# Four crossed tiles instead of seven on TensorE, a gather released every 5.85 products, and another order of the first block

## The chip, the cores and the metric

One NeuronCore of one Trainium2 chip runs the kernel. The metric is the device time of a whole run in microseconds. The kernel before has a median of 119.67 us over three runs. A difference of about 0.2% is what such a measurement can tell from no change.

## What is computed

A recommender model on 2048 samples: eight embedding fields, a wide part with two crossed fields, and three dense layers.

```python
S = [s0, s1, s2, s3, s4, s5, s6, s7]   # indices of 2048 samples
E = [E0, ..., E7]                      # tables of (125000, 25000, 12500, 375, 375, 1000, 500, 100) x 64
w = [w0, ..., w7]                      # one weight per table row
wide = dense @ Wd_wide                 # dense: 2048 x 13
for si, wi in zip(S, w):
    wide = wide + wi[si]
wide = wide + wc0[S[3] * VOCABS[4] + S[4]]   # 375 x 375 entries
wide = wide + wc1[S[5] * VOCABS[6] + S[6]]   # 1000 x 500 entries
deep_in = jnp.concatenate([dense @ Wd_deep] + [Ei[si] for Ei, si in zip(E, S)], axis=1)
h = jax.nn.relu(deep_in @ W1)          # 576 -> 512
h = jax.nn.relu(h @ W2)                # 512 -> 256
return bias + h @ W3 + wide            # 256 -> 1
```

## The kernel before, in words

The 2048 samples are four blocks of 512, and a block is four tiles of 128. Every large product is made of float32 operands split into a high and a low fp32r part: hi x hi, hi x lo and lo x hi, so three matmuls of 512 columns each (L901, L902, L903 in `product`).

**Two ways to a table row.** Fields 0, 1 and 2 have large tables; GpSimd gathers their rows with indirect DMAs (L388), one for each tile and field: 12 per block, 48 in all (8 `x_pair` for fields 0 and 1, and 4 `x_two` for field 2, per block). The five small tables are looked up on TensorE: VectorE builds a one-hot matrix of the indices (`build_onehot`, L569, 19 chunks of 128 rows per block) and TensorE multiplies the table with it (`look_up`, L842). The weights of the wide part are looked up in the same way by `look_up_wide` (19 narrow matmuls, L854).

**The crossed fields.** The first one, wc0, is a table of 375 x 375. A tile of it can be gathered by GpSimd (L401), or be done on TensorE, a *crossed tile*: six matmuls of 376 columns pick the row (`look_up_crossed`, L893), and VectorE picks the column and sums (`take_crossed`, L684). XTILES = 7 tiles of the 16 go this way, at the places of the table CROSSED, written (block, place). For them TensorE also spreads the row indices (L877, one 128-column matmul a tile). The remaining 9 tiles of wc0 and all 16 of wc1 are gathered, 25 in all.

**When a gather starts.** GpSimd issues its gathers in one fixed order. Those of block 0 start as soon as the indices are there: first four `x_two`, then eight `x_pair` with a memset of 160 columns (`pause`, L376) behind each. All later ones wait for the semaphore `gather_released`. TensorE raises it: `count` adds up the products issued (1 for a 512-column matmul, less for a narrower one), and when a matmul marked free finds the sum above PACED_FROM + PACE x (gathers released so far), 58 + 6.3 n, its end releases one gather. Look-ups' last matmuls, the low-weight matmuls of `product`, turns and the wide look-up are not free.

**The first block.** TensorE starts with five filler matmuls (L1013), spreads the indices of block 0 over the partitions (L826), runs two more fillers (BUSY), and then follows an order written out by hand. ScalarE copies the spread indices (`copy_spread`, L410; field 5's is the fifth, into `idx_bc`), splits the high halves of the tables (L463) and weights (L467), and copies each look-up's result out of PSUM (L429, L430). VectorE computes the low halves of the tables (L579) and weights (L575) between the one-hots. The dense features have a weight product of their own, Wd_deep x W1 (L1030), which `dense` (L958) uses.

**The later blocks** repeat one order in a loop: layer 2, look-ups, layer 1 by groups of 128 input rows, turns of the gathered rows (L866), the crossed tiles at their places. Three PSUM banks (`io_ps`) go round among look-ups, turns, crossed tiles and sums. The last block ends with layer 2 in two halves, the matmuls L997 and L1006, and on VectorE the sum of the crossed gathers (L797), the result of three blocks (L798) and the final add (L801).

## Time and profile before

| | |
|---|---|
| median of three runs | 119.67 us (119.65 to 119.74) |
| the profiled execution, its own time | 119.41 us |
| its span in the profile | 117.6 us |
| TensorE busy | 113.9 us, 97% of the span |
| VectorE, ScalarE, GpSimd busy | 77.2, 57.8, 80.8 us |
| DMA moved | 7.47 MB, 64 GB/s on average |

The profile's times start at the span's start. A row of a timeline has the start, the length, the engine, the source line, the operation, output and input, and in brackets the idle time before it with what ended it. Matmuls overlap: their starts follow each other closer than their lengths tell. The chain of waits is followed back from the last instruction, at each step to what released it.

### The profile page before, as it was taken

The page shows a single profiled execution, that of the slowest core. Times are in us where ns is not written, and L with a number is a line of the kernel's source. Part 1 is how long each engine was busy: PE and PEld are TensorE (multiplying, and loading weights), DVE is VectorE, ACT ScalarE, POOL GpSimd, SP SyncE. Part 2 cuts the span into 40 slices and gives each one's busy share as a digit, 9 for nine tenths or more (in the row PEclk, how much of TensorE's full clock was granted, in tenths as well). Part 3 has the DMA queues.
Part 4 walks back from the last instruction along what each step waited for, and adds up shares of the span by engine and source line. Part 5 has one row for each costly group of instructions (what it writes and reads, how often), then busy time and mean ns, then how long its engine had stood idle before and what let it go on. Part 6 is the DMA issues. An engine that isn't in the chain of part 4 may idle for free.

```text
span 117.6 us, 1749 instructions
## 1 busy us (share of the span) xinstructions
PE 113.9 (97%) x595; PEld 89.0 (76%) x595; DVE 77.2 (66%) x195; ACT 57.8 (49%) x106; POOL 80.8 (69%) x92
## 2 busy tenths in 40 slices
PE   5999999999999999999999999999999999999992
PEld 2757665877887886888888886788888888688892
DVE  3799999948999944929994504847997004534450
ACT  5799977169593251238255052407628052406230
POOL 7578888575787773667777768377777766377630
PEclk9999999999999999999999999999999999999999
DMA  2897954459732343033334442120000000000000
GB/s 72 244 213 268 232 149 85 82 149 279 271 25 20 21 85 27 5 27 25 28 23 71 36 26 23 11 21 3 0 9 0 0 0 0 0 0 0 6 0 3
DMA packets 6073, 7.47 MB, mean 64 GB/s; under 512 B 2748, under 2 KB 3772, under 8 KB 6064
## 3 DMA queue, kind: packets, MB, share of 16 engines
q0 software_dynamic: 2336, 1.61, 17.2%
q1 hardware_dynamic: 3728, 5.74, 14.9%
q8 instruction: 5, 0.08, 0.3%
q14 instruction: 4, 0.03, 0.1%
HBM read 7.32 MB, written 0.03 MB: 62 GB/s over the span
## 4 chain that ended last, share of the span: by engine, by line
PE 88%; DVE 5%; ACT 2%; DMA 2%; issue 0%
PE l_ps L901 18%; PE l_ps L903 18%; PE l_ps L902 18%; PE io_ps L842 12%; PE io_ps L893 6%; PE io_ps L854 4%; DVE onehot L569 3%; PE l_ps L958 3%; PE io_ps L866 2%; PE l_ps L826 2%; DMA idx_raw<-in_index_dram 2%; PE io_ps L983 1%; ACT xt_lo L430 1%; ACT xt_hi L429 1%; PE io_ps L997 1%; PE io_ps L1013 1%
## 5 line engine op out<-in xcount | busy, mean ns | idle before, releaser
L388 POOL DMA_INDIRECT x_pair<-in_rows_dram,idx_gather x32 | 33.5, 1048 | 13.3 <-issue 5.1
L569 DVE TENSOR_SCALAR onehot<-idx_bc,row_id 128x512 fp32r<-128x512 f16 x76 | 33.0, 496 | 2.3 <-PE io_ps L854 2.1
L401 POOL DMA_INDIRECT cross<-in_wc_dram,idx_cross x25 | 24.8, 990 | 10.3 <-issue 4.9
L901 PE MATMUL l_ps<-xt_hi,w_hi 128*128 128x512 f32 x60 | 23.9, 398 | 0.0
L903 PE MATMUL l_ps<-xt_hi,w_lo 128*128 128x512 f32 x60 | 23.6, 393 | 0.0
L902 PE MATMUL l_ps<-xt_lo,w_hi 128*128 128x512 f32 x60 | 23.5, 391 | 0.0
L388 POOL DMA_INDIRECT x_two<-in_rows_dram,idx_gather x16 | 17.6, 1097 | 7.7 <-issue 3.7
L842 PE MATMUL io_ps<-onehot,table_hl 128*128 128x512 f32 x76 | 21.4, 405 | 0.2 <-DVE onehot L569 0.2
L429 ACT CAST xt_hi<-io_ps 64x512 fp32r<-64x512 f32 x20 | 11.6, 579 | 16.2 <-PE io_ps L842 16.0
L842 PEld LDWEIGHTS io_ps<-onehot,table_hl 128*128 128x128 f32 x76 | 14.2, 189 | 5.1 <-issue 1.3
L459 ACT ACTIVATE h<-l_ps 128x512 f32<-128x512 f32 (+2 forms) x10 | 5.0, 512 | 21.5 <-PE l_ps L903 21.5
L901 PE MATMUL l_ps<-h_hi,w_hi 128*128 128x512 f32 (+1 forms) x36 | 13.4, 372 | 0.0
L901 PEld LDWEIGHTS l_ps<-xt_hi,w_hi 128*128 128x128 f32 x60 | 11.3, 188 | 2.8 <-issue 0.5
L903 PE MATMUL l_ps<-h_hi,w_lo 128*128 128x512 f32 (+1 forms) x36 | 13.3, 369 | 0.0
L902 PE MATMUL l_ps<-h_lo,w_hi 128*128 128x512 f32 (+1 forms) x36 | 13.2, 366 | 0.0
L903 PEld LDWEIGHTS l_ps<-xt_hi,w_lo 128*128 128x128 f32 x60 | 11.3, 188 | 2.5
L902 PEld LDWEIGHTS l_ps<-xt_lo,w_hi 128*128 128x128 f32 x60 | 11.3, 188 | 2.4
L590 DVE TENSOR_TENSOR xt_lo<-io_ps,xt_hi 128x512 fp32r<-128x512 f32 x4 | 2.8, 692 | 15.2 <-ACT xt_hi L443 15.2
L623 DVE SCALAR_TENSOR_TENSOR h_lo<-l_ps,h_hi 128x512 fp32r<-128x512 f32 x16 | 10.1, 682 | 3.9 <-ACT h_hi L450 3.9
L430 ACT CAST xt_lo<-io_ps 64x512 fp32r<-64x512 f32 x20 | 11.6, 582 | 0.5
L450 ACT ACTIVATE h_hi<-l_ps 128x512 fp32r<-128x512 f32 x16 | 8.8, 598 | 4.0 <-PE l_ps L903 3.6
L684 DVE SCALAR_TENSOR_TENSOR taken<-col_id,cross_col,io_ps 128x376 f32<-128x376 f32 x7 | 4.2, 602 | 8.6 <-PE io_ps L893 8.6
(101 smaller groups left out, 140.7 us busy)
## 6 DMA issues: line engine op xcount, KB each, us to landing
idx_bc<-idx_dram SPq DMA_DIRECT2D x3, 640.0 KB, 7.2
w_sb<-in_w_dram SPq DMA_DIRECT2D x4, 256.0 KB, 4.6
dense_x<-in_dense_x_dram SPq DMA_DIRECT2D x4, 154.0 KB
table<-in_wc_rows_dram SPq DMA_DIRECT2D x1, 564.0 KB, 3.8
x_pair<-in_rows_dram,idx_gather POOLq DMA_INDIRECT x32, 3.5
w_sb<-in_w_dram SPq DMA_DIRECT2D x1, 512.0 KB, 4.3
cross<-in_wc_dram,idx_cross POOLq DMA_INDIRECT x25, 2.4
table<-in_small_dram SPq DMA_DIRECT2D x1, 256.0 KB, 3.5
```

The source lines that it names most:

```text
L388: nc.gpsimd.indirect_dma_start(out=x_two[:, t // 2, t % 2 * ROW:(t % 2 + 1) * ROW] if f == 2 else x_pair[:, t, f * ROW:(f + 1) * ROW], out ...
L401: nc.gpsimd.indirect_dma_start(out=cross[:, c, t:t + 1], out_offset=None, in_=wc[c], in_offset=bass.IndirectOffsetOnAxis(ap=idx_cross[:, c ...
L429: nc.scalar.copy(xt_hi[b % 2][to, g, :], bank[0:D, :]).then_inc(io_act, 1)
L430: nc.scalar.copy(xt_lo[b % 2][to, g, :], bank[D:2 * D, :]).then_inc(io_act, 1)
L450: nc.scalar.activation(h1_hi[:, m, :], l1_ps[m][:], ACT.Relu).then_inc(l1_high, 1)
L569: nc.vector.tensor_scalar(onehot[:, CHUNK0[i] + c, :], idx_bc[:, b % (BLOCKS - 1), i, :], row_id[:, c:c + 1], None, ALU.is_equal).then_inc ...
L623: nc.vector.scalar_tensor_tensor(out=h1_lo[:, m, :], in0=l1_ps[m][:], scalar=0.0, in1=h1_hi[:, m, :].bitcast(f32), op0=ALU.max, op1=ALU.su ...
L842: last = count(nc.tensor.matmul(io_bank(use)[:], table_hl[:, c, :], onehot[:, c, :], start=c == CHUNK0[i], stop=ends), free=not ends)
L893: last = count(nc.tensor.matmul(io_bank(use)[:, 0:XPAD], row_onehot[:, c, t % BT * P:(t % BT + 1) * P], cross_hl[:, part, c, :], start=c + ...
L901: count(nc.tensor.matmul(dst, w_hi, a_hi, start=start, stop=False), columns, free=True)
L902: count(nc.tensor.matmul(dst, w_hi, a_lo, start=False, stop=False), columns, free=True)
L903: return count(nc.tensor.matmul(dst, w_lo, a_hi, start=False, stop=stop), columns)
```

## The change

- XTILES goes from 7 to 4. The crossed tiles stand at (1, 3), (2, 1), (2, 3), (3, 1); those at (1, 1), (1, 2), (2, 0), (2, 2) are gone and (2, 1) is new. Three more tiles of wc0 are gathered, so there are 28 cross gathers.
- The gathers are released by other numbers: the eight `x_pair` gathers of block 0 too, at 9 + 5.6 n products, and the rest every 5.85 products. The memsets between the first gathers are gone.
- In block 0 the two fillers before the first look-up are gone; the dense weights' product is issued before look-up (0, 1), and its inputs are loaded earlier; ScalarE's copy of W1's group 2 stands behind the third index copy; VectorE computes the low half of W1's group 3 behind the last one-hots, and then the parts of the wide weights; TensorE takes group 3's matmuls with high weights first (`layer1_weights_low_last`); `dense(0)` is issued before `turn(0, 0)`.

The diff, cut to its core:

```diff
--- before.py
+++ after.py
@@ -45,35 +45,32 @@
-BUSY = 2
...
-XTILES = 7
+XTILES = 4
...
-PAUSE = 160
-PACE, PACED_FROM = 6.3, 58
...
-CROSSED = {(1, 1): [0], (1, 2): [1], (1, 3): [2], (2, 0): [3], (2, 2): [4], (2, 3): [5],
-           (3, 1): [6]}
+PACE, FIRST_PACE, PACED_FROM = 5.85, 5.6, 9
+
+FIRST_RELEASED = BT * 2
+RELEASED = FIRST_RELEASED + (BLOCKS - 1) * BT * NG + NX * TILES - XTILES
...
+CROSSED = {(1, 3): [0], (2, 1): [1], (2, 3): [2], (3, 1): [3]}
...
-RELEASED = (BLOCKS - 1) * BT * NG + NX * TILES - XTILES
@@ -303,10 +299,10 @@
             table_part(0)
-            w1_part(2)
-            table_part(1)
             sp.dma_start(wd_rep[:], wd_rep_t).then_inc(wd_loaded, 16)
             sp.dma_start(w1d_sb[:], w1[0:D, :]).then_inc(wd_loaded, 16)
+            table_part(1)
+            w1_part(2)
             table_part(2)
@@ -369,20 +365,14 @@
-            def pause(n, columns):
-
-                if n:
-                    pool.wait_ge(paused, n)
-                nc.gpsimd.memset(pause_sb[:, 0:columns], 0.0).then_inc(paused, 1)
-
...
-                            if b > 0:
+                            if b > 0 or f != 2:
                                 released += 1
                                 pool.wait_ge(gather_released, released)
...
-                            if b == 0 and f != 2:
-                                pause(pauses, PAUSE)
-                                pauses += 1
@@ -475,9 +462,9 @@
-            weight_high(2)
             table_high_part(1)
             copy_spread(2)
+            weight_high(2)
             copy_spread(3)
@@ -732,11 +719,8 @@
             table_low_part(2)
+            build_onehot(0, 4, range(4, CHUNKS[4]))
             w1_low_part(1)
-            build_onehot(0, 4, range(4, CHUNKS[4]))
-            w1_low_part(2)
-            wdense_low()
-            turned_lo(0, 1)
...
+            w1_low_part(2)
+            turned_lo(0, 1)
+            wdense_low()
             dense_low(0)
@@ -813,10 +800,13 @@
+            def release_at(n):
+                return PACED_FROM + FIRST_PACE * min(n, FIRST_RELEASED) + PACE * max(n - FIRST_RELEASED, 0)
+
...
-                if free and work[0] >= PACED_FROM + PACE * released[0] and released[0] < RELEASED:
+                if free and released[0] < RELEASED and work[0] >= release_at(released[0]):
@@ -915,15 +905,28 @@
+            def layer1_weights_low_last(g):
+
+                pe.wait_ge(io_act, act_count(IO_AT["look", 0, 3]))
+                pe.wait_ge(w1_high, W1_ORDER.index(g) + 1)
+                for m in range(M1):
+                    for part in (xt_hi[0], xt_lo[0]):
+                        count(nc.tensor.matmul(l1_ps[m][:], w1_hi[:, g, m * P:(m + 1) * P], part[:, g, :],
+                                               start=False, stop=False), free=True)
+                pe.wait_ge(w1_low, W1_ORDER.index(g) + 1)
+                for m in range(M1):
+                    count(nc.tensor.matmul(l1_ps[m][:], w1_lo[:, g, m * P:(m + 1) * P], xt_hi[0][:, g, :],
+                                           start=False, stop=False), free=True)
@@ -1022,24 +1025,23 @@
-            keep_busy(BUSY, io_ps[1])
             look_up(0, 0)
-            look_up(0, 1)
             pe.wait_ge(wd_loaded, 32)
             pe.wait_ge(row_index_ready, 1)
             nc.tensor.matmul(l2_ps[0:NROWS, :], wd_rep[:], w1d_sb[:], start=True, stop=True).then_inc(wdense_done, 1)
+            look_up(0, 1)
             look_up(0, 2)
...
-            layer1(0, 3)
+            layer1_weights_low_last(3)
             look_up_wide(0)
             layer1(0, 1)
             look_up(1, 0)
+            dense(0)
             turn(0, 0)
-            dense(0)
             look_up(1, 1)
```

GpSimd's queue from the first gathers to the row gathers of block 1, before:

```order
L371 MEMSET ones 128x1
L388 DMA x_two<-in_rows_dram,idx_gather 128x65 x4
L388 DMA x_pair<-in_rows_dram,idx_gather 128x65
L376 MEMSET pause_sb 128x160
...
L388 DMA x_pair<-in_rows_dram,idx_gather 128x65 x8
L388 DMA x_two<-in_rows_dram,idx_gather 128x65 x4
```

And after:

```order
L367 MEMSET ones 128x1
L378 DMA x_two<-in_rows_dram,idx_gather 128x65 x4
L378 DMA x_pair<-in_rows_dram,idx_gather 128x65 x16
L378 DMA x_two<-in_rows_dram,idx_gather 128x65 x4
L378 DMA x_pair<-in_rows_dram,idx_gather 128x65 x8
```

The memsets are gone, and the sixteen row gathers of blocks 0 and 1 wait alike for `gather_released`.

VectorE's queue around the last one-hots of block 0, before (L569 one-hots, L579 and L575 low halves of tables and weights):

```order
L569 TENSOR_SCALAR onehot<-idx_bc,row_id 128x512 x5
L579 TENSOR_TENSOR table_hl<-table,table_hl 128x8x64
L575 TENSOR_TENSOR w_lo<-w_sb,w_hi 128x512
L569 TENSOR_SCALAR onehot<-idx_bc,row_id 128x512 x4
L575 TENSOR_TENSOR w_lo<-w_sb,w_hi 128x512
L610 TENSOR_TENSOR wdense_hl<-l_ps,wdense_hl 13x512
L595 TENSOR_TENSOR xt_lo<-io_ps,xt_hi 64x2x128 x2
```

And after (L556, L566 and L562 are the same three lines):

```order
L556 TENSOR_SCALAR onehot<-idx_bc,row_id 128x512 x5
L566 TENSOR_TENSOR table_hl<-table,table_hl 128x8x64
L556 TENSOR_SCALAR onehot<-idx_bc,row_id 128x512 x4
L562 TENSOR_TENSOR w_lo<-w_sb,w_hi 128x512
L727 CAST look_w_parts<-look_w 128x19
L728 TENSOR_TENSOR look_w_rest<-look_w,look_w_parts 128x19
L729 CAST look_w_parts<-look_w_rest 128x19
L730 TENSOR_TENSOR look_w_parts<-look_w_rest,look_w_parts 128x19
L562 TENSOR_TENSOR w_lo<-w_sb,w_hi 128x512
```

The four last one-hots now follow the table's low half directly, and the weights' low half and the four steps on the wide weights come behind them.

TensorE's queue in block 0, from the index spreads to the second layer-1 products, before:

```order
L826 MATMUL l_ps<-ident,idx_look 128x128 x4
L1013 MATMUL io_ps<-zero 128x512 x2
L842 MATMUL io_ps<-onehot,table_hl 128x512 x6
L1030 MATMUL l_ps<-w1d_sb,wd_rep 77x512
L842 MATMUL io_ps<-onehot,table_hl 128x512 x4
L912 MATMUL l_ps<-xt_hi,w_hi 128x512 x2
```

And after:

```order
L816 MATMUL l_ps<-ident,idx_look 128x128 x4
L832 MATMUL io_ps<-onehot,table_hl 128x512 x3
L1031 MATMUL l_ps<-w1d_sb,wd_rep 77x512
L832 MATMUL io_ps<-onehot,table_hl 128x512 x7
L902 MATMUL l_ps<-xt_hi,w_hi 128x512 x2
```

The two fillers went out, and the dense weights' product stands between the first three look-up matmuls and the other seven.

## Rows read from the trace of the kernel before

**Rows 1.** The page: busy us, share of the span and instructions of the engines.
```profile
PE 113.9 (97%) x595; PEld 89.0 (76%) x595; DVE 77.2 (66%) x195; ACT 57.8 (49%) x106; POOL 80.8 (69%) x92
```

**Rows 2.** The chain of waits, 5 to 16.5 us: start, us, engine, output, line.
```profile
8.67 0.58 ACT xt_hi L429
...
9.88 0.59 ACT idx_bc L410
...
10.49 2.06 DVE onehot L569 x4
...
13.14 0.60 DVE w_lo L575
...
15.81 0.51 PE io_ps L842
```

**Rows 3.** The timeline of TensorE in block 0: start, us, line, operation, tiles, count.
```profile
3.66 1.01 PE L826 MATMUL l_ps<-ident,idx_look 128*128 128x128 f16 x8 [0.15 <-DVE idx_look L554]
...
8.04 1.08 PE L1030 MATMUL l_ps<-w1d_sb,wd_rep 64*77 64x512 f32 x2
9.05 1.19 PE L842 MATMUL io_ps<-onehot,table_hl 128*128 128x512 f32 x4
...
19.10 1.32 PE L854 MATMUL io_ps<-onehot,look_w_parts 128*32 128x512 bf16 x19
...
23.94 0.60 PE L866 MATMUL io_ps<-ident,x_pair 128*128 128x128 f32 x4
...
26.01 0.72 PE L912 MATMUL l_ps<-xt_hi,w_hi 128*128 128x512 f32 x2
```

**Rows 4.** VectorE: its timeline, and L569 alone from 10.4 to 15.9 us (ns).
```profile
4.90 2.47 DVE L569 TENSOR_SCALAR onehot<-idx_bc,row_id 128x512 fp32r<-128x512 f16 x6
...
18.71 0.25 DVE L746 TENSOR_TENSOR look_w_parts<-look_w_rest,look_w_parts 128x19 bf16<-128x19 f32 x1
...
L569 DVE TENSOR_SCALAR onehot<-idx_bc,row_id x8: 469/530/772, 10.5 to 15.0; 128x512 fp32r<-128x512 f16 x8
```

**Rows 5.** The timeline of GpSimd: a pause, the last row gather of block 0, and the end.
```profile
12.29 0.42 POOL L376 MEMSET pause_sb<- 128x160 f32 x1
...
20.36 0.97 POOL L388 DMA_INDIRECT x_pair<-in_rows_dram,idx_gather  x1 [0.16 <-issue]
...
102.75 0.94 POOL L401 DMA_INDIRECT cross<-in_wc_dram,idx_cross  x1 [2.02 <-PE l_ps L958]
...
111.77 0.94 POOL L401 DMA_INDIRECT cross<-in_wc_dram,idx_cross  x1 [0.31 <-PE l_ps L901]
```

**Rows 6.** The chain of waits at the index spreads and at a crossed tile.
```profile
35.85 0.41 PE io_ps L877 x7
...
44.12 1.04 PE io_ps L893 x6
```

**Rows 7.** The page's groups of gathers: busy, mean ns, idle before.
```profile
L388 POOL DMA_INDIRECT x_pair<-in_rows_dram,idx_gather x32 | 33.5, 1048 | 13.3 <-issue 5.1
...
L401 POOL DMA_INDIRECT cross<-in_wc_dram,idx_cross x25 | 24.8, 990 | 10.3 <-issue 4.9
...
L388 POOL DMA_INDIRECT x_two<-in_rows_dram,idx_gather x16 | 17.6, 1097 | 7.7 <-issue 3.7
```

**Rows 8.** Who waited for whom: us in total, times, longest.
```profile
DVE taken L684 <- PE io_ps L893: 8.6, 5, 2.3
...
PEld io_ps L866 <- DMA x_pair<-in_rows_dram,idx_gather: 0.2, 1, 0.2
```

**Rows 9.** The line L401: from a cross gather's start to its landing.
```profile
DMA to landing us min/median/max: 2.3/2.4/3.3
```

**Rows 10.** The timeline of VectorE at the end.
```profile
114.22 0.18 DVE L797 TENSOR_TENSOR wide_cross<-wide_bias,cross 128x16 f32<-128x16 f32 x1 [0.34 <-DMA cross<-in_wc_dram,idx_cross]
114.43 0.17 DVE L798 TENSOR_TENSOR result<-wide_cross,deep 128x12 f32<-128x12 f32 x1
115.52 0.16 DVE L801 TENSOR_TENSOR result<-wide_cross,io_ps 128x4 f32<-128x4 f32 x1 [0.92 <-PE io_ps L1006]
```

15 lines of the change are left out of this document (7 added, 8 removed).

## The prediction

> **What bounds the kernel now.** I read the busy shares first. TensorE is busy for 113.9 of 117.6 us [rows 1]: there is hardly a hole to fill, so time comes off there only with its work. The chain of waits says the same, with one exception. From 6 to 16 us it does not run on TensorE, although TensorE reads as busy: it runs from the first look-ups over ScalarE's copies (the second pair starts at 8.67) and the last index copy (L410, 9.88) to VectorE, which then builds eight one-hots (L569) with two low halves (L579, L575) between them; TensorE's last look-up matmul waits for the last one-hot, at 15.81 [rows 2]. From there on TensorE's own stream is the path up to the final add at 115.52 [rows 10]. GpSimd's gathers are a second, nearly full queue: 48 row gathers and 25 cross gathers [rows 7]. The profiled run took 119.41 us, 1.8 more than its span and 0.26 less than the median of 119.67; I take the change from the span and apply it to the median.
>
> **Part 1, three crossed tiles less on TensorE.** One crossed tile is six matmuls and holds the chain for 1.04 us [rows 6]. Three fewer give 3 x 1.04 = 3.12 us. Seven index spreads in one stretch hold it for 0.41 us [rows 6], so three fewer give 0.18. Nothing else waits behind them: in each place where a tile goes, the next group of TensorE (a layer-1 group, the wide look-up, look-up (2, 1)) has inputs that were ready earlier, since VectorE waited there for the crossed product and not the reverse (8.6 us over five waits, [rows 8]). The tile that moves to place (2, 1) costs what it did. Sum: **-3.3 us**; bounds -3.1 (the spreads hidden) and -3.5 (three switches of shape more, of some 0.05 each, go as well).
>
> **Part 2, the start of block 0.** Its steps, in order of time:
> - The two filler matmuls go. Look-up (0, 0) can start behind the spreads: 3.66 + 21 x 0.107 is about 5.9. Its first matmul, of 512 columns, still runs at the lower clock, 0.43 us: up to there eight 128-column matmuls take 1.01 us, later seven hold the chain for 0.41 [rows 3, 6], which is the lower (1.2 GHz) against the upper level (2.4 GHz). The clock should rise by 6.4 as today, so its third matmul starts at about 6.62.
> - The product of the dense weights (L1030) now comes before look-up (0, 1). It holds the queue for 9.05 - 8.04 = 1.01 us [rows 3]. It starts at 6.62 + 0.32 = 6.94, look-up (0, 1) starts at 7.95 and its last matmul is done at 8.90 (four of them take 1.19 us, so three about 0.95). ScalarE's copies of it started at 8.67 [rows 2] and now start near 8.93: **+0.27**, and the copy L410, for which VectorE waits, comes that much later. The order of ScalarE's earlier copies is turned round without a change of their sum. Bounds 0 and +0.5.
> - The low half of W1's group 3 (L575, 0.60 us in the chain, [rows 2]) moves behind the last one-hot: **-0.60**. TensorE does not need it at once, since the new order takes eight matmuls of high weights first (8 x 0.23 = 1.8 us). This is safe.
> - The memsets on GpSimd between the gathers go. Undisturbed, six one-hots take 2.47 us, or 0.40 each beside the next start; in the critical stretch the longest takes 772 ns, and the median 530 [rows 4]. The first four of the stretch end at 12.55, just over the start of a memset at 12.29 [rows 5], and the second four have such a meeting too; the first six one-hots ran beside gathers and show nothing of the kind. Four one-hots that start 0.40 apart end after 3 x 0.40 + 0.47 = 1.67 us instead of 2.06 [rows 2], and the second four are as long, since they end just before 15.81: up to 2 x 0.39 = -0.78. I take **-0.65**, because a gather may still touch one; bounds 0 and -0.78.
> - Behind that, layer 1's group 1 waits less: the wide look-up started only at 19.10, behind its weights' parts, which were done at 18.96 [rows 3, 4]; they are now built earlier: **-0.1**.
> - The eight row gathers of block 0 are now released by TensorE instead of being issued between memsets. Counting products (0.25 for a wide matmul), the eighth is released by the first matmul behind the wide look-up, at about 19.6, and starts near 20.0. A gather that started at 20.36 had landed when the turn began at 23.94, with some 0.2 us of waiting [rows 3, 8], so this takes 3.4 to 3.6 us; the new one lands at 23.4 to 23.7, and the turn, now behind the dense product, comes up at about 23.7. **+0.1**; bounds 0 and +0.5.
>
> Sum of part 2: 0.27 - 0.60 - 0.65 - 0.1 + 0.1 = **-1.0 us**. Layer 1 of group 0, at 26.01 today [rows 3], should start near 25.0. All at the good end gives -1.4, all at the bad end +0.3.
>
> **Part 3, the gathers behind.** Three cross gathers more, 28 instead of 25, all on GpSimd, and paced at 5.85 products. Undisturbed, a gather with the 0.31 before it takes 0.94 + 0.31 = 1.25 us, and with the disturbed ones among them 1.29 (cross) to 1.40 (x_two) [rows 5, 7]. A release comes every 5.85 x 0.23 = 1.35 us and more where uncounted work lies between, so the queue can just follow. In the last block TensorE frees none during the wide look-up and the turns; the queue runs dry and starts again at 102.75, today with eight gathers to go, of which the eighth starts at 111.77 [rows 5]. Now nine are to go: on today's axis the ninth starts at 102.75 + 8 x 1.25 = 112.75 and has landed 2.4 us later [rows 9], at 115.15. VectorE's L797 waits for that; it and L798 need 0.21 and about 0.1 before the engine is free [rows 10], so 115.5, where the final add starts today at 115.52 because of TensorE. The cover of 0.9 us is used up. **+0.05**; bounds 0 and +0.9 (a landing of 3.3 us, [rows 9]).
>
> **Sum.** -3.3 - 1.0 + 0.05 = -4.25 us. From the profiled 119.41 that is 115.2, from the median **115.4 us**.
>
> **A rule weighed.** GpSimd's gathers run beside VectorE's one-hots, and their mean is 1.05 us over 32, against 0.94 for one alone [rows 5, 7]. The Trainium skill (SBUF — State Buffer, section Who interferes with whom) says that a VectorE instruction in a two-port mode and a GpSimd instruction exclude each other, and the same page (A bandwidth-pool intuition that's wrong) gives some 620 ns alone against 3100 ns overlapped for such a DMA. By that rule the memsets' removal frees VectorE, as I assume; but it also speaks against adding gathers. By its figure, an estimate, 72 gathers would need over 220 us, so the trace disagrees with its size.
>
> **Rivals.**
> - *A, the start gives nothing.* The dense product ahead of look-up (0, 1) delays VectorE by 0.5, the one-hots stay long for another reason (gathers now start where memsets did), and the turn waits 0.5 for its rows: 0.5 - 0.6 - 0.1 + 0.5 = +0.3. For it: ScalarE's copies are gapless from 8.67 on, so whatever they start late reaches VectorE whole [rows 2]. Against: the memset's coincidence with the long one-hot. Time 119.67 - 3.3 + 0.3 = 116.7; half-way, with the memsets' part missing only, 116.0.
> - *B, the last gather ends the kernel.* The ninth gather starts or lands late by 0.5 to 1 us more: 115.9 to 116.4. For it: its cover is gone by my own sum. Against: landings have a median of 2.4.
> - *C, the clock.* Without fillers the rise to the full level comes later. Each 512-column matmul then takes 0.43 instead of 0.23 and the dense product twice 1.01; through ScalarE's chain that costs 1 to 1.5 us: 116.4 to 116.9. Against: look-ups fill the place of the fillers without a hole.
> - *D, slower than before: GpSimd becomes the bound from end to end.* 72 released gathers start at about 10.0. By kind they take 32 x 1.35 + 12 x 1.40 + 28 x 1.29 = 96.1 us [rows 7], so the last would end at 106, before TensorE. The kernel gets slower than today only if the last one starts after 112.9 of the span, which needs a mean of (112.9 - 10.0) / 71 = 1.45 us against 1.33. At 1.48 the last starts at 115.1 and the time is about 121.9. It needs every gather lengthened by 0.15. The rule weighed above would point this way.
> - *E, the change doesn't do what it says.* The counts of instructions rule that out for the crossed tiles.
>
> **How the numbers follow.** Forecast 0.62; A, half or whole, 0.18; B 0.10; C 0.05; D 0.02; an even better start 0.03. The likeliest is 115.4. The low end takes the good end of part 2 and of part 1: 119.67 - 3.5 - 1.4 = 114.8. The high end takes in A and most of C: 116.8. About 0.2% is what a measurement here can tell from no change: slower by more only with D, 0.02; within it 0.01; faster 0.97.
>
> **What would show it.** In the new profile: 24 matmuls of crossed tiles at 1.04 us per six; the last look-up matmul of block 0 near 14.8; no one-hot above 0.6 us between 10 and 16 us; group 0 of layer 1 near 25.0; the span near 113.3; the final add released by TensorE with L797 just ahead of it. A last look-up matmul near 15.5 means that the memsets were not the cause (A). A wait of the final add for L797 or a DMA means B. 128-column or 512-column matmuls at half speed behind 7 us mean C. GpSimd without idle time from 10 us on means D.

## The result, and the profile after

The changed kernel takes 116.8 us (median of 6 runs, 115.8 to 119.7) where the kernel before takes 119.7: the ratio is 0.968 [0.967, 0.970]. The ratio leaves out runs that were disturbed or over 1.5% above the fastest, and here that matters: of the twelve runs of the changed kernel in two sittings seven lie between 115.4 and 117.0 us and five between 117.6 and 119.7, while the kernel before stays within 119.4 and 120.3. Forecast was 115.4 with a range of 114.8 to 116.8. The direction holds, and the median lies on the upper end of the range; as the runs scatter over 3.9 us and the second sitting gave 116.84, that it falls inside is partly luck. 115.4 is the best run, not the median. The profiled run took 117.59 us, 1.8 more than its span of 115.8.

The page after: the engines, and the three groups of gathers (line, engine, operation, tiles, count; busy us, mean ns; idle time before).

```profile
PE 110.4 (95%) x572; PEld 85.2 (74%) x572; DVE 73.1 (63%) x186; ACT 57.2 (49%) x105; POOL 84.7 (73%) x87
...
L378 POOL DMA_INDIRECT x_pair<-in_rows_dram,idx_gather x32 | 35.2, 1100 | 12.3 <-issue 7.0
L388 POOL DMA_INDIRECT cross<-in_wc_dram,idx_cross x28 | 27.8, 992 | 8.5 <-issue 4.6
...
L378 POOL DMA_INDIRECT x_two<-in_rows_dram,idx_gather x16 | 19.6, 1228 | 5.9 <-issue 3.0
```

TensorE lost 3.5 us of work [rows 1], as it should. GpSimd's gathers take 6.7 us more than before, 82.6 against 75.9, although three gathers at 0.99 make only 3.0: the others have become longer too, x_pair 1100 ns against 1048, x_two 1228 against 1097 [rows 7]. TensorE's timeline in block 0 and at the end, after:

```profile
13.13 0.44 PE L856 MATMUL io_ps<-ident,x_two 128*128 128x128 f32 x2 [0.22 <-DMA x_two<-in_rows_dram,idx_gather]
13.33 2.11 PE L832 MATMUL io_ps<-onehot,table_hl 128*128 128x512 f32 x8
15.28 0.40 PE L924 MATMUL l_ps<-xt_hi,w_hi 128*128 128x512 f32 x1
...
18.10 1.32 PE L844 MATMUL io_ps<-onehot,look_w_parts 128*32 128x512 bf16 x19
...
24.21 0.66 PE L856 MATMUL io_ps<-ident,x_pair 128*128 128x128 f32 x4 [0.18 <-DMA x_pair<-in_rows_dram,idx_gather]
25.29 1.20 PE L832 MATMUL io_ps<-onehot,table_hl 128*128 128x512 f32 x3 [0.42 <-ACT xt_lo L417]
26.32 0.62 PE L902 MATMUL l_ps<-xt_hi,w_hi 128*128 128x512 f32 x2
...
111.07 0.95 PE L1000 MATMUL io_ps<-ones,wide_deep_look 128*128 128x1 f32 x8
```

The wide look-up starts at 18.10 instead of 19.10 [rows 3]: the microsecond is won there. Eight us later it is gone: layer 1 of group 0 starts at 26.32 instead of 26.01 [rows 3], because the turn at 24.21 waited for its gathers and the look-up behind it for ScalarE (how much each took is told below, at the run with the memsets). The second loss stands at the end. VectorE's timeline there, then the last entries of the chain of waits (start, us, engine, output, line):

```profile
113.42 0.17 DVE L784 TENSOR_TENSOR wide_cross<-wide_bias,cross 128x16 f32<-128x16 f32 x1 [2.56 <-DMA cross<-in_wc_dram,idx_cross]
...
113.72 0.15 DVE L788 TENSOR_TENSOR result<-wide_cross,io_ps 128x4 f32<-128x4 f32 x1
```

```profile
109.75 1.01 POOL cross L388
110.76 0.30 issue
111.07 2.33 DMA cross<-in_wc_dram,idx_cross
```

In the kernel before the final add waited 0.92 us for TensorE and L797 0.34 for a DMA [rows 10]. Now L784, the same operation, waits 2.56 us for the last cross gather, and the final add follows it at once. Where TensorE ends the kernel, the add starts 1.44 us after L1000 (110.61 and 112.05 in the run with the split row, below; L997, the same, at 114.09 and the add at 115.52 before), so TensorE would have allowed 111.07 + 1.44 = 112.51. The add started at 113.72: **1.21 us** are lost to the gather.

So the difference of spans adds up: TensorE's stretch from layer 1 of group 0 to L1000 fell from 114.09 - 26.01 = 88.08 to 111.07 - 26.32 = 84.75, **-3.33**; the start of that stretch **+0.31**; the end **+1.21**. Together -1.81, and the span went from 117.6 to 115.8.

### The profile page after: what moved, and what is told of

Read it like the earlier page. It is cut to its first block, busy times and chain, and to the rows that moved or that the text cites. A ratio compares the mean times of both kernels' runs of the same rounds, so it can differ in the third digit from the quotient of the medians.

```text
span 115.8 us, 1680 instructions
## 1 busy us (share of the span) xinstructions
PE 110.4 (95%) x572; PEld 85.2 (74%) x572; DVE 73.1 (63%) x186; ACT 57.2 (49%) x105; POOL 84.7 (73%) x87
## 4 chain that ended last, share of the span: by engine, by line
PE 72%; DMA 16%; SPq 4%; ACT 2%; POOL 2%; issue 1%; DVE 0%; DVEq 0%
PE l_ps L891 16%; PE l_ps L893 16%; PE l_ps L892 15%; PE io_ps L832 11%; DMA w_sb<-in_w_dram 5%; DMA idx_bc<-idx_dram 4%; DMA idx_dram<-row_idx 4%; PE io_ps L883 4%; PE io_ps L844 3%; PE l_ps L961 2%; DMA cross<-in_wc_dram,idx_cross 2%; PE io_ps L856 2%; POOL cross L388 2%; PE io_ps L986 2%; SPq L296 1%
## 5 line engine op out<-in xcount | busy, mean ns | idle before, releaser
L378 POOL DMA_INDIRECT x_pair<-in_rows_dram,idx_gather x32 | 35.2, 1100 | 12.3 <-issue 7.0
L388 POOL DMA_INDIRECT cross<-in_wc_dram,idx_cross x28 | 27.8, 992 | 8.5 <-issue 4.6
L556 DVE TENSOR_SCALAR onehot<-idx_bc,row_id 128x512 fp32r<-128x512 f16 x76 | 31.7, 482 | 2.2 <-PE io_ps L844 2.0
L378 POOL DMA_INDIRECT x_two<-in_rows_dram,idx_gather x16 | 19.6, 1228 | 5.9 <-issue 3.0
L891 PE MATMUL l_ps<-xt_hi,w_hi 128*128 128x512 f32 x56 | 22.3, 398 | 0.0
L893 PE MATMUL l_ps<-xt_hi,w_lo 128*128 128x512 f32 x56 | 22.0, 393 | 0.0
L892 PE MATMUL l_ps<-xt_lo,w_hi 128*128 128x512 f32 x56 | 21.9, 392 | 0.0
L891 PEld LDWEIGHTS l_ps<-xt_hi,w_hi 128*128 128x128 f32 x56 | 10.5, 188 | 2.7 <-issue 0.4
L893 PEld LDWEIGHTS l_ps<-xt_hi,w_lo 128*128 128x128 f32 x56 | 10.5, 188 | 2.3
L892 PEld LDWEIGHTS l_ps<-xt_lo,w_hi 128*128 128x128 f32 x56 | 10.5, 188 | 2.3
L417 ACT CAST xt_lo<-io_ps 64x512 fp32r<-64x512 f32 x20 | 11.7, 583 | 0.5
L891 PEld LDWEIGHTS l_ps<-h_hi,w_hi 128*128 128x128 f32 x36 | 6.8, 189 | 1.4 <-issue 0.4
```

Source lines behind the costliest of these rows:

```text
L378: nc.gpsimd.indirect_dma_start(out=x_two[:, t // 2, t % 2 * ROW:(t % 2 + 1) * ROW] if f == 2 else x_pair[:, t, f * ROW:(f + 1) * ROW], out ...
L388: nc.gpsimd.indirect_dma_start(out=cross[:, c, t:t + 1], out_offset=None, in_=wc[c], in_offset=bass.IndirectOffsetOnAxis(ap=idx_cross[:, c ...
L417: nc.scalar.copy(xt_lo[b % 2][to, g, :], bank[D:2 * D, :]).then_inc(io_act, 1)
L556: nc.vector.tensor_scalar(onehot[:, CHUNK0[i] + c, :], idx_bc[:, b % (BLOCKS - 1), i, :], row_id[:, c:c + 1], None, ALU.is_equal).then_inc ...
L891: count(nc.tensor.matmul(dst, w_hi, a_hi, start=start, stop=False), columns, free=True)
L892: count(nc.tensor.matmul(dst, w_hi, a_lo, start=False, stop=False), columns, free=True)
```

## The experiments

Three questions: what each half of the change is worth alone, what eats the microsecond of the start, and what makes the last gather late. The time of the kernel before beside each was 119.6 to 119.7 us.

**The change once more.** No edit.

> The changed kernel once more, for a second profile. Theory 1 (a chain of long gathers, one of 3.70 us and one of 2.87 us, filled GpSimd's queue in the first profile, and the last gather set the end 1.95 us late): an execution without such gathers has a span near 113.9 us and the final add released by TensorE; one with them ends behind the last cross gather. Theory 2 (the pace itself is too fast for the queue): the last gather sets the end in every execution, also with no gather above 1.5 us. Ratio to before 0.966 to 0.971.

116.84 us (115.44 to 118.57), ratio 0.972 [0.967, 0.977]. In its profile (115.88 us, span 114.1) group 0 starts at 25.75, the last gather at 109.24 and L1000 at 110.56, 84.81 behind group 0. The add comes 1.43 us after L1000, and no gather takes over 1.92 us, as theory 1 has it. The 84.8 us come again, the two other terms don't: they vary from run to run.

**The crossed tiles alone.**

```diff
-XTILES = 7
+XTILES = 4
-PACE, PACED_FROM = 6.3, 58
+PACE, PACED_FROM = 5.85, 53.8
-CROSSED = {(1, 1): [0], (1, 2): [1], (1, 3): [2], (2, 0): [3], (2, 2): [4], (2, 3): [5],
-           (3, 1): [6]}
+CROSSED = {(1, 3): [0], (2, 1): [1], (2, 3): [2], (3, 1): [3]}
```

> The kernel before with the new tile table and the new pace alone (XTILES 4, release base 53.8 and 5.85 products); its first block and its memsets stay. Prediction: -3.3 us of TensorE and +0.05 to +0.9 at the tail, so 116.4 us, ratio 0.973. Rival (first block gives nothing, all of the gain is the tiles): ratio 0.968, 115.9 us.

118.34 us (116.9 to 119.2), ratio 0.985 [0.981, 0.989]: about half of the 3.3 us, and slower than both expectations. TensorE's stretch is as short as it should be, 111.51 - 26.72 = 84.79 us. Its timeline, then the end of VectorE's:

```profile
26.72 0.73 PE L911 MATMUL l_ps<-xt_hi,w_hi 128*128 128x512 f32 x2
...
111.51 0.95 PE L996 MATMUL io_ps<-ones,wide_deep_look 128*128 128x1 f32 x8
```

```profile
113.91 0.18 DVE L796 TENSOR_TENSOR wide_cross<-wide_bias,cross 128x16 f32<-128x16 f32 x1 [2.60 <-DMA cross<-in_wc_dram,idx_cross]
...
114.20 0.15 DVE L800 TENSOR_TENSOR result<-wide_cross,io_ps 128x4 f32<-128x4 f32 x1
```

The add could have come at 111.51 + 1.44 = 112.95 and came at 114.20: the last gather takes back 1.25 us. The other 0.7 are the start of group 0, 26.72 here and 26.01 before with the same code, which is that run's. In this kernel alone 2.4 to 2.9 us of each run lie outside the span, 1.8 in all others; that takes another 0.6 to 1 us and is not explained.

**The new first block alone.** Seven tiles and the old spacing of later gathers, the rest of the diff.

> The kernel before with the new first block alone: XTILES 7, the old tile table, the old pace of 6.3 from product 58 for the later gathers. Prediction: -1.0 us, 118.7 us, ratio 0.992. Rival (W2's load lands late, at 22.4 us in the first profile of the changed kernel, and takes all of it back): 119.7 us, ratio 1.000.

120.34 us (118.8 to 122.6), ratio 0.999 [0.996, 1.002]. The ratio is the rival's, its reason is not: layer 2's weights reach ScalarE at 20.64 here. The wide look-up starts at 17.91, and then the turn of block 0 waits. TensorE's timeline, and the stretches around it (each engine's busy us and count; PEclk is the granted clock, 1.00 the upper level of 2.4 GHz and 0.50 the lower of 1.2):

```profile
22.76 1.08 PE L962 MATMUL l_ps<-dense_hl,wdense_hl 77*128 77x512 f32 x4
26.48 0.86 PE L857 MATMUL io_ps<-ident,x_pair 128*128 128x128 f32 x4 [2.64 <-DMA x_pair<-in_rows_dram,idx_gather]
26.99 1.63 PE L833 MATMUL io_ps<-onehot,table_hl 128*128 128x512 f32 x3
28.42 1.05 PE L903 MATMUL l_ps<-xt_hi,w_hi 128*128 128x512 f32 x2
```

```profile
26.00:28.00 2.00, 1.52 (x7) 1.32 (x7) 0.01 (x1) 0.58 (x1) 0.35 (x1) 0.70 0.55 30
28.00:30.00 2.00, 2.00 (x6) 1.60 (x5) 1.62 (x3) 1.16 (x2) 0.94 (x1) 0.50 0.75 228
```

TensorE idles 2.6 us, the clock falls to the lower level at 26.8 and comes back at 30.2, and two matmuls take 1.05 us where they take 0.62 after. (The Trainium skill, TensorE: Matmul & The Clock Gate, section HAM oscillation — how this bites in real kernels, says that a wait for a DMA can send the clock back to the lower level; this trace agrees.) A stretch of 3.4 us at the lower level in a span of 120.8 is a mean clock of 0.986. The four slowest of these 14 runs, 121.6 to 122.6 us, have just that mean, and so have, at 0.985, the two slowest without the three gathers and the slowest at spacing 5.4 (both below, 118.7 to 118.9 us); the three slowest of the changed kernel have 0.975 to 0.981. The mean alone does not tell the place, though. The kernel with breaks (below) has 0.984 in its profile and waited only 0.30 us at the turn: its clock is at the lower level from 112.8 us to the end, behind TensorE's last matmul, while the add waits for the last gather. All but one of these slowest runs had no profile. That they wait at the turn is inferred, and is likely only where no late gather ends the kernel: here and without the three gathers.

Why the gathers are late shows on GpSimd, here the last three of block 0:

```profile
19.02 1.49 POOL L379 DMA_INDIRECT x_pair<-in_rows_dram,idx_gather  x1 [0.30 <-issue]
20.82 0.95 POOL L379 DMA_INDIRECT x_pair<-in_rows_dram,idx_gather  x1 [0.30 <-issue]
22.07 1.78 POOL L379 DMA_INDIRECT x_pair<-in_rows_dram,idx_gather  x1 [0.30 <-PE l_ps L892]
```

The eighth starts at 22.07, not near 20.0 as forecast, and takes 1.78 us beside VectorE's w_lo of 1024 columns.

**The same, with the gathers of block 0 released by nothing.**

```diff
-                            if b > 0 or f != 2:
+                            if b > 0:
                                 released += 1
-            work, released = [0.0], [0]
+            work, released = [0.0], [FIRST_RELEASED]
```

> The kernel before with the new first block alone (seven tiles, old spacing of later gathers), and the eight x_pair gathers of block 0 released by nothing: GpSimd issues them back to back behind the x_two ones. The new first block alone had come to 120.3 us (ratio 0.9988 of before), with TensorE waiting 2.64 us for those gathers at its turn of block 0 and then 3.4 us at the lower clock. Theory A (the order of the first block is worth what was predicted, about 1 us, and TensorE's releases give it back, because a released gather that meets VectorE's one-hots is too late for the turn): no wait over 0.3 us at the turn of block 0, layer 1's first step of group 0 begins at 25.0 to 25.6 us (26.01 before), full clock throughout, time 118.5 to 119.2 us, ratio 0.990 to 0.996. Theory B (the new order itself is worth nothing: look-up 1 and the weights that it brings forward wait for other loads instead): the turn without a wait, but group 0 at 25.8 to 26.3 us and the time 119.4 to 120.0 us, ratio 0.998 to 1.003.

119.01 us, ratio 0.996 [0.993, 0.998]. The twelve runs fall into two heaps: nine at 118.7 to 119.2, three at 120.0 to 120.1. The profile caught one of the three:

```profile
25.34 0.66 PE L857 MATMUL io_ps<-ident,x_pair 128*128 128x128 f32 x4 [1.36 <-DMA x_pair<-in_rows_dram,idx_gather]
```

No wait over 0.3 us was expected. Here the eighth gather started at 20.96 and took 2.02 us, since the back-to-back gathers at 12.6 and 14.4 had met one-hots too (1.48 and 1.80). The wait of 1.4 is the distance of the heaps, 1.2. The nine are 0.8 us below the kernel before, which would be the worth of the new order when the turn waits little; none of them was profiled, so that is inferred from the distance. Their time is theory A's, but a free issue does not by itself mend the wait. These runs come from another sitting than those of the new first block alone.

**The memsets put back** behind block 0's x_pair gathers, these released by nothing, everything else as changed.

```diff
+                            if b == 0 and f != 2:
+                                if pauses:
+                                    pool.wait_ge(paused, pauses)
+                                nc.gpsimd.memset(pause_sb[:, 0:160], 0.0).then_inc(paused, 1)
+                                pauses += 1
```

> The changed kernel with the memsets of 160 columns back behind block 0's eight x_pair gathers, and these gathers not released by TensorE; all the rest as changed. If the memsets lengthen the one-hots: two one-hots of some 0.77 us again between 10 and 16 us, the last look-up matmul of block 0 0.6 to 0.8 us later, and the kernel up to 0.65 us slower than the changed one (ratio to before 0.974). If they do not: same one-hots and the same time within 0.2 us.

116.79 us (116.0 to 117.4), ratio 0.975 [0.971, 0.979]. The one-hots of 10 to 15 us (ns: shortest, median, longest), with the memsets, then after, without:

```profile
L562 DVE TENSOR_SCALAR onehot<-idx_bc,row_id x8: 467/512/772, 10.4 to 14.5; 128x512 fp32r<-128x512 f16 x8
```

```profile
L556 DVE TENSOR_SCALAR onehot<-idx_bc,row_id x9: 469/476/542, 9.9 to 14.0; 128x512 fp32r<-128x512 f16 x9
```

The memsets do lengthen them, and four take 2.0 us again. Yet layer 1 of group 3 starts at 15.39 against 15.28 after, as if only 0.1 of the 0.65 reached TensorE. That pair misleads, because TensorE's turn at 13.13 in the profile of after waited for x_two rows and held up the look-up behind it. From the start of the last index copy, for which VectorE waits, to group 3 it is 6.27 us in the kernel before, 4.93 to 5.41 (mean 5.04) in the ten profiles with the new order and no memsets, and 5.56 and 5.63 in the two with memsets. So the memsets cost TensorE about 0.55 us.

The turn of block 0 has no wait here, and group 0 starts at 25.28, 1.04 before the profile of after. The turn comes 5.76 us behind the wide look-up instead of 6.11, and group 0 1.28 us behind the turn instead of 2.11. So 0.35 of the loss after belong to the gathers and 0.83 to the look-up that waited for ScalarE, which was late with layer 2's weights (more on them at the three edits together). At the end this kernel loses 1.22 us like the changed one: L1006, the same as L1000, starts at 110.04 and the add at 112.70.

**Released by nothing, without memsets.** The two edits that released block 0's gathers above (`if b > 0` and `released` from FIRST_RELEASED on), in the changed kernel.

> The changed kernel with block 0's eight x_pair gathers neither released by TensorE nor spaced by memsets. If their release is what makes the turn wait (0.16 and 0.18 us in two profiles, 2.64 us in the one of the first block alone): they end by about 20 us instead of 22, the turn starts behind the dense product with no wait, and layer 1 of group 0 starts at 25.2 instead of 25.8; ratio to the changed kernel 0.997. If the gathers then meet the one-hots of 10 to 15 us and lengthen them: those one-hots above 0.5 us, and no gain.

116.82 us (115.6 to 118.4), ratio 0.970 [0.965, 0.974]. No wait at the turn, group 0 at 25.59. Yet the span is 115.0: L1000 starts at 110.33, which allows the add at 111.77, and it came at 112.93. So a good start alone is not enough; the last gather, at 110.33, takes 1.16 us.

**Three cross gathers less.** The last three of the second crossing are left out (their columns are zero).

> The changed kernel without its last three cross gathers (three tiles of wc1 are left out of the sum and read as zero); everything else as changed, so GpSimd's queue ends three gathers, 3.75 us, earlier. Theory 1 (the spread and the median above the fast runs come from the last gather landing late): all runs close together at the fast level, 115.5 to 116.0 us, ratio 0.967, and the final add released by TensorE. Theory 2 (the spread comes from the first block's loads and turn): the spread stays, 115.5 to 119.

117.15 us (115.7 to 118.9), and the spread stays, as theory 2 has it. Now nothing waits for a gather at the end:

```profile
111.73 0.17 DVE L785 TENSOR_TENSOR wide_cross<-wide_bias,cross 128x16 f32<-128x16 f32 x1
...
113.46 0.16 DVE L789 TENSOR_TENSOR result<-wide_cross,io_ps 128x4 f32<-128x4 f32 x1 [1.35 <-PE io_ps L1010]
```

But the turn of block 0 waited 1.34 us and group 0 started at 27.27. Each cause suffices for a run above 117.

**Releases closer together.**

```diff
-PACE, FIRST_PACE, PACED_FROM = 5.85, 5.6, 9
+PACE, FIRST_PACE, PACED_FROM = 5.4, 5.6, 9
```

> The changed kernel with later gathers released every 5.4 products instead of 5.85. Theory 1: the last release comes 0.45 x 63 = 28 products, 6.5 us, earlier, so GpSimd works with no idle time from block 1 on and has 1 to 2 us more at its end to take up long gathers: median 116.0 to 116.4 us. Theory 2 (the queue is full anyway, and earlier releases bring nothing): 116.8 us.

116.53 us (115.4 to 118.9), between the two theories; the ratio of 0.976 [0.972, 0.980] shows no gain over the changed kernel. The profile has the shortest span of all, 113.6: last gather at 108.79, add at 111.51, exactly where TensorE allows it (110.08 + 1.44 = 111.52).

**Why the last gather is late.** VectorE and GpSimd around 48 us in the changed kernel:

```profile
48.17 3.25 DVE L556 TENSOR_SCALAR onehot<-idx_bc,row_id 128x512 fp32r<-128x512 f16 x8
```

```profile
47.29 0.94 POOL L378 DMA_INDIRECT x_pair<-in_rows_dram,idx_gather  x1 [0.30 <-PE l_ps L961]
48.54 3.70 POOL L378 DMA_INDIRECT x_pair<-in_rows_dram,idx_gather  x1 [0.30 <-issue]
52.54 0.95 POOL L378 DMA_INDIRECT x_pair<-in_rows_dram,idx_gather  x1 [0.30 <-PE l_ps L892]
```

The gather starts 0.37 us into an unbroken row of eight one-hots and takes 3.70 us, until 0.8 after the row. Another, 1.7 us into the row at 35.70, took 2.87. The longest in the kernel before is 1.79. (The Trainium skill, SBUF — State Buffer, section Who interferes with whom, has the one that comes second blocked for the other's whole instruction, and the same page, section A bandwidth-pool intuition that's wrong, gives 620 against 3100 ns. The prediction set that figure aside, because the mean of before was 1.05 us. The excess of this one gather, 2.8 us, is near the page's 2.5, an estimate from its two figures. But a single one-hot lasts 0.48 us, so a block for one instruction doesn't give it, and as a mean over all gathers the figure doesn't hold.) From 48.54 on GpSimd has no idle time but the 0.30 between gathers, and it never runs dry. In the last block, after:

```profile
99.77 0.94 POOL L388 DMA_INDIRECT cross<-in_wc_dram,idx_cross  x1 [0.30 <-PE l_ps L961]
...
111.07 0.94 POOL L388 DMA_INDIRECT cross<-in_wc_dram,idx_cross  x1 [0.30 <-issue]
```

Before, there were 2.02 us of idle time ahead of 102.75 [rows 5]. A gather takes 1.25 us and a release comes every 1.35, so each of the some 45 gathers behind 52 us gives back a tenth of a microsecond at most. The profiles bear this out. In the four with both long gathers the last one starts 84.7 to 84.8 us behind group 0, in the four with neither 83.4 to 83.5, and in the one with the 3.7 alone and closer releases 83.5. The difference, 1.3 us, is about one gather, and it makes the 1.2 us lost at the end.

**Small breaks in the rows.** Behind every second one-hot of blocks 1 to 3 a VectorE addition of one column:

```diff
+                    if b > 0 and c % 2 == 1:
+                        nc.vector.tensor_tensor(gap_sb[:, n:n + 1], wd_scratch[:, 0:1], wd_scratch[:, 1:2], ALU.add)
```

> The changed kernel with a tensor_tensor of one column on VectorE behind every second one-hot of blocks 1 to 3, so that the rows of eight one-hots are no longer one behind the other. Theory 1 (a gather that begins its write inside such a row is locked out until the row ends: 37.41 to 40.28 and 48.54 to 52.24 us in the first profile): no gather above 1.6 us in these rows, median at 115.6 to 116.2 us, little spread. Theory 2 (long gathers come from the DMA side or from chance): gathers of 2.8 and 3.7 us remain and the time is that of the changed kernel, 116.8 us.

119.33 us, ratio 0.994 [0.991, 0.998]: the gain is nearly gone. The gather is as long as ever (47.60, 3.77 us), though it starts 0.19 us ahead of its row, and another joins it (74.54, 3.91). In the profile the add came at 114.47, 2.5 us after TensorE allowed it. The additions start before the one-hot ahead of them has ended (48.58 and 48.66), and VectorE has no idle time in the row, so the run doesn't test a row with real holes.

```profile
47.60 3.77 POOL L379 DMA_INDIRECT x_pair<-in_rows_dram,idx_gather  x1 [0.30 <-issue]
```

**The row split by a wait.**

```diff
                 if b + 2 < BLOCKS:
+                    dve.wait_ge(io_full, IO_AT["look", b + 2, 0] + 1)
                     build_onehot(b + 2, 2)
```

> The changed kernel, with one wait added on VectorE in blocks 0 and 1: between the one-hots of look-up 1 and those of look-up 2 of the block after the next (the row of eight at 48.2 to 51.4 us) VectorE waits for TensorE to have filled the bank of that block's look-up 0. The row falls into 3 and 5, as it did in the kernel before, whose fourth tile stood there (2.29 us of waiting between). Theory A (a gather that starts just after VectorE has begun an unbroken row of one-hots is held until the row is over, and the 2.5 us that it loses at 48.5 us are still missing from GpSimd's queue at the end): the gather at about 48.5 us takes at most 1.3 us in place of 3.70, no gather after 40 us takes over 1.5, GpSimd's last gather starts at 109.5 us or earlier (111.07 in the first profile of the changed kernel), and the time is 115.3 to 116.3 us. The gather of 2.87 us at 37.4 stays, since the row of eight at 35.7 is untouched. Theory B (the gather's 3.70 us are memory or queue trouble and have nothing to do with the row): it stays at 3.5 us or more. Theory C (GpSimd catches up anyway, TensorE's releases set the last gather): gathers short, but the last one still at 110.5 to 111.1 us and the time 116.5 to 117. Against both: if the added wait makes VectorE late for the rounded hidden rows at 53.8 us, the kernel is 0.3 to 1 us slower than the changed one.

116.16 us (115.5 to 116.8), ratio 0.971 [0.967, 0.975]; the last gather starts at 109.27 and TensorE ends the kernel again. The time and three of the four numbers of theory A came true, and still the profile does not prove it. The gather that was to stay at 2.87 us took 1.27, though its row was not touched: the backlog was gone before the split row came. VectorE, then GpSimd:

```profile
47.72 1.27 DVE L556 TENSOR_SCALAR onehot<-idx_bc,row_id 128x512 fp32r<-128x512 f16 x3
50.27 2.09 DVE L556 TENSOR_SCALAR onehot<-idx_bc,row_id 128x512 fp32r<-128x512 f16 x5 [1.28 <-PE io_ps L833]
```

```profile
46.34 0.94 POOL L378 DMA_INDIRECT x_pair<-in_rows_dram,idx_gather  x1 [1.34 <-PE l_ps L962]
47.59 1.18 POOL L378 DMA_INDIRECT x_pair<-in_rows_dram,idx_gather  x1 [0.30 <-issue]
```

The gather started 0.13 us before the row, not 0.37 into it, and the second profile of the changed kernel has the same meeting with the row of eight left whole:

```profile
47.66 3.25 DVE L556 TENSOR_SCALAR onehot<-idx_bc,row_id 128x512 fp32r<-128x512 f16 x8
```

```profile
46.28 0.94 POOL L378 DMA_INDIRECT x_pair<-in_rows_dram,idx_gather  x1 [1.37 <-PE l_ps L961]
47.52 1.19 POOL L378 DMA_INDIRECT x_pair<-in_rows_dram,idx_gather  x1 [0.30 <-issue]
```

At this place the length goes with the phase. Where GpSimd had run dry and was released by the dense product (the idle 1.34 and 1.37 us above), the next gather starts 0.13 us ahead of the row and takes 1.2 us: in that profile, in the three with a split row, in the one with three gathers less, in the kernel before and in the two with seven tiles. Where it still had a backlog it starts 0.37 into the row and takes 3.7: in the first profile of the changed kernel, with the tiles alone, with the memsets, released by nothing, and with closer releases, five of five.

That the phase alone decides is not shown, for two reasons. The gather of the kernel with breaks started 0.19 us ahead of its row and took 3.77 all the same. And in the row of eight at 35.7 a gather starts 0.40 us in and takes 1.00, in all thirteen traces but that of the kernel with breaks. Here from the first profile of the changed kernel:

```profile
35.70 3.26 DVE L556 TENSOR_SCALAR onehot<-idx_bc,row_id 128x512 fp32r<-128x512 f16 x8
```

```profile
36.10 1.00 POOL L378 DMA_INDIRECT x_two<-in_rows_dram,idx_gather  x1 [0.30 <-PE l_ps L892]
37.41 2.87 POOL L378 DMA_INDIRECT x_two<-in_rows_dram,idx_gather  x1 [0.30 <-issue]
```

Either 0.03 us make the difference or something else does, such as the kind of gather (x_two here, x_pair at 48.54); no run tells them apart. The backlog in four of the five comes from the gather of 2.87 us at 37.4. That one starts 1.70 us into its row in all four traces that have it, and in nine others, the kernel before among them, a gather starts at the same 1.70 and takes 1.28. So its cause is open; and a split row met by a gather 0.37 us into it was not seen.

**Three edits together:** released by nothing, the row split, and layer 2's weights no longer behind block 1's spread indices:

```diff
-            sp.wait_ge(index_spread[1], 16)
             sp.wait_ge(w1_low, 2)
```

> The changed kernel with three edits together: block 0's x_pair gathers released by nothing; the row of eight one-hots split by a wait for TensorE as in the run beside it; and the load of layer 2's weights issued behind the second low part of layer 1's weights alone, no longer behind the landing of block 1's spread indices. Theory A (the changed kernel lost at three places: the turn of block 0 that waits for released gathers, 0.2 to 3 us; the one-hots that hold a gather, 2.5 us on GpSimd; layer 2's weights that land at 22.4 and make ScalarE late for look-up 1 of block 1, 0.4 to 0.6 us): turn of block 0 with no wait, layer 1's group 0 at 25.0 to 25.4 us, last gather at 109 us or earlier, time 114.6 to 115.4 us, and little spread between runs. Theory B (TensorE's later work sets the end, about 111.8 us for its last product, and an earlier start only moves a wait behind it): 115.6 to 116.5 us. If GpSimd's back-to-back gathers of block 0 collide with the earlier load of layer 2's weights, group 0 stays at 26 us.

116.32 us (115.4 to 117.1). Theory A failed at the turn: 1.39 us of waiting as in the free first block above (gathers of 1.88, 1.80 and 2.02 us), group 0 at 26.92, span 115.3. The last gather started at 110.37, about as late as TensorE's late end could bear. The time is theory B's, but as the start was not earlier, B is not tested. The weights were issued at 15.63 against 15.59 with the wait in the run beside it, so that wait cost nothing. In the first profile of after they reached ScalarE at 22.44, where the thirteen others have 19.2 to 21.0:

```profile
22.44 1.05 ACT L484 CAST w_hi<-w_sb 128x1024 fp32r<-128x1024 f32 x1 [4.35 <-DMA w_sb<-in_w_dram]
```

The load took 6.3 us from issue to landing there and 4.3 in the second profile. ScalarE's copies behind it ran late one after the other, up to `xt_lo` (L417), for which the look-up at 25.29 waited. Why that one load was slow is open.

**Memsets back and the row split.**

> The changed kernel with the memsets back behind the x_pair gathers of block 0, those gathers released by nothing, and the row of eight one-hots split by the wait for TensorE. Each edit alone gave 116.8 and 116.2 us of median (before 119.6), the second with fewer runs over 117 us. Theory A (what scatters the runs of the changed kernel between 115.5 and 119.7 us is the race between GpSimd's gathers and VectorE's rows at two places: the last gather of block 0, for which TensorE's turn waits up to 2.6 us, and the gather held at 48.5 us): both places are mended here, so the turn of block 0 has no wait, layer 1's group 0 begins at 25.1 to 25.5 us, no gather after 40 us takes over 1.5 us, the last one starts by 109.4 us, and the six runs lie within 1.2 us of each other, with their median at 115.4 to 116.2. Theory B (the first block's one-hots, made long again by the memsets, cost what the turn's wait gives back, and the rest of the spread has another cause): median 116.4 to 116.9, with runs over 117.

115.93 us (115.4 to 116.9), ratio 0.970 [0.966, 0.973]: the best median of all. TensorE's timeline and the end of VectorE's:

```profile
24.52 0.60 PE L863 MATMUL io_ps<-ident,x_pair 128*128 128x128 f32 x4
24.88 0.94 PE L839 MATMUL io_ps<-onehot,table_hl 128*128 128x512 f32 x3
25.80 0.73 PE L909 MATMUL l_ps<-xt_hi,w_hi 128*128 128x512 f32 x2
...
110.53 0.95 PE L1007 MATMUL io_ps<-ones,wide_deep_look 128*128 128x1 f32 x8
```

```profile
111.65 0.18 DVE L791 TENSOR_TENSOR wide_cross<-wide_bias,cross 128x16 f32<-128x16 f32 x1 [1.33 <-DMA cross<-in_wc_dram,idx_cross]
...
111.97 0.16 DVE L795 TENSOR_TENSOR result<-wide_cross,io_ps 128x4 f32<-128x4 f32 x1
```

No wait at the turn, and the add is where TensorE allows it (110.53 + 1.44). The median is within theory A's bounds; the spread is 1.4 us where 1.2 was said, one gather behind 40 us took 1.71 where 1.5 was the limit, and group 0 missed its 25.1 to 25.5 by 0.3, as the wide look-up already started at 18.75. Of the 18 runs with a split row none is above 117.1; of the 36 of the other kernels with four tiles and the new first block, breaks left aside, thirteen are. That does not show that the split takes such runs away. All 18 come from other sittings than the 36, their ratios to the kernel before (0.970 to 0.971) are those of the changed kernel (0.968 and 0.972), and the kernel with three gathers less kept its spread although no gather could end it late.

## Why the prediction was right, and where not

- **Part 1, -3.3 us: right to 0.05.** From layer 1 of group 0 to L1000 it is 88.08 us before and 84.73 to 84.81 in all eleven profiles with four tiles, however late the group started. Nothing waited behind the removed tiles.
- **Part 2, -1.0: the steps held as far as the wide look-up, the sum did not.** In twelve profiles with the new order the wide look-up starts at 17.6 to 18.8, mean 18.25, against 19.10 and 19.83 with the old one: -0.85 to -1.2. By step: the last index copy starts at 10.28 in the mean (9.83 to 10.88) against 9.88 and 10.25, so +0.4 or +0.03 where +0.27 was said. From that copy to group 3 it is -1.23 (5.04 against 6.27) where -0.60 and -0.65 were said; the memsets' part of it is about 0.55. (All steps at their good end make -1.5, not the -1.4 of the text.)
- **The step that failed there is the turn's wait**, put at +0.1 with bounds 0 and +0.5. From the wide look-up to group 0 it is 6.9 us with the old order, 7.05 where the turn has no wait (with the memsets, with memsets and the split row, released by nothing), and 7.4 to 8.7 in eight others, 10.5 in one. The prediction counted when TensorE would release the eighth gather and took it to start then, at 20.0, with a gather's time alone. It forgot the queue: without memsets the gathers come back to back, some of those beside one-hots and w_lo take 1.4 to 2.0 us instead of 0.95, and the eighth starts at 20.6 to 22.1 in nine profiles of ten. With the memsets it starts at 19.9 and 20.1 and the turn doesn't wait; but in one of the three profiles without memsets and without a release it didn't either, so they are not the only way. Worse, the longest wait cost the clock, 3.4 us at the lower level, which rival C looked for at 7 us and not here.
- **A wait that the prediction did not have:** in the profile of after 0.83 us are lost to ScalarE, behind a slow load of layer 2's weights, and only 0.35 to the turn. In the other profiles it doesn't come.
- **Part 3, +0.05, was mis-sized; its bound of +0.9 was passed in the profiled run, 1.21.** That it could come so was rival B. The step that failed is "the queue runs dry and starts again at 102.75". The idle time there, 2.02 us before, is still 0.96 to 0.98 in four profiles (the three with a split row and the one with three gathers less); the six with a gather of 3.7 us and the second one of after have none. Its own start of the last gather, 112.75 - 4.25 = 108.5, compares with 108.8 to 109.3 in the good profiles and 110.0 to 111.8 in the others. That held gathers make the difference is shown by the profiles; what holds them is not.
- **Together for the profiled run:** forecast span 113.35, measured 115.8; +1.32 from group 0 (25.0 forecast, 26.32), +1.16 from the end. For the median it is 1.4 us, between the good runs and this one. The four profiles with the end free and at most 0.41 us of waiting at the turn took 115.4 to 115.9 us.
- **Rivals.** A was right that the turn can wait 0.5 and more, and wrong on the one-hots: the memsets did lengthen them. B came true in five of the ten profiles with four tiles and all gathers. Each had been priced as if the other did not come. C's rise was on time (the dense product at 6.66 takes 1.08 us, as at 8.04 before); the clock fell elsewhere. D was wrong: the mean spacing stayed below 1.45 us, though with 1.43 in the kernel with breaks and in that of after GpSimd ran near the edge.

## What to carry to other kernels

When gathers share GpSimd's queue with VectorE's work beside them, cost them one by one at the place where they will run and carry the backlog forward; a mean over the kernel hides the few that are held for two or three microseconds. Filler work on a queue that spaces gathers can be what keeps a consumer from waiting, so before it is removed, look at who waits for the last gather, not only at whom the filler slows. If a change makes the best run faster but the runs scatter, read two profiles of it before explaining either.

## What the runs showed of the hardware

- A gather that started 0.37 us into a row of eight back-to-back one-hots (3.25 us) took 3.70 us in five traces of five, one that started 0.13 us ahead of the row 1.2 us. But one that started 0.40 us into another such row took 1.00 us in thirteen of thirteen, and with one-column instructions between the one-hots one that started 0.19 us ahead took 3.77. Not explained.
- Two gathers with the same start in the same row, 1.70 us into it, took 2.87 us in four traces and 1.28 in nine. Not explained.
- Memsets of 160 columns on GpSimd (0.25 to 0.45 us each) lengthened VectorE's one-hots beside them from 476 to 512 ns in the median, and the longest from 542 to 772.
- After 2.6 us of waiting TensorE's granted clock was at the lower level for 3.4 us; after 1.3 to 1.4 us of waiting, in three traces, it stayed at the upper.
- It is also at the lower level behind TensorE's last matmul in some runs (from 112.8 to 116.6 us in the kernel with breaks, a mean of 0.984), where no matmul is left to slow down; a low mean does not show a wait in the middle.
